# One block from attention to the experts, and batch 0's input rows reloaded in four portions

## The reference

```python
scores = einsum('bqhd,bkhd->bhqk', q, k) / sqrt(16) + slopes * -abs(pos_k - pos_q)
out = einsum('bhqk,bkhd->bqhd', softmax(scores), v) @ Wout + bout
x = layernorm(x + out)
# router: softmax over 8 logits, the top 2 kept; each expert takes its first 512 tokens
h = relu(einsum('ceh,ehi->cei', inputs, experts_inter))         # 256 -> 1024
out = einsum('cei,eih->ceh', h, experts_out) * in_w             # 1024 -> 256
x = layernorm(x + combined)
```

## Time and profile before

| | us |
|---|---|
| three runs: lowest, median, highest | 1104.36, 1107.05, 1108.21 |
| the profiled execution, its own time | 1107.38 |
| its span, first to last instruction | 1105.6 |
| attention, first score matmul to last value matmul | 116.41 to 815.35 |
| routing, first matmul to the slot table | 826.22 to 880.71 |
| experts, first gather to the end | 882.07 to 1105.6 |

### The profile page before, as it was taken

The page is one execution under the profiler, slowest core; times in us unless marked ns, Lnnn a source line. Parts: engine busy times, 40 slices in busy tenths (PEclk is TensorE's granted clock), DMA queues, the critical chain, the costliest instruction groups (busy, mean ns, idle before and its releaser), DMA issues. The chain is left out here.

```text
span 1105.6 us, 38348 instructions
## 1 busy us (share of the span) xinstructions
PE 1035.5 (94%) x16912; PEld 678.4 (61%) x16912; DVE 434.4 (39%) x1016; ACT 822.8 (74%) x832; POOL 304.1 (28%) x454
## 2 busy tenths in 40 slices
PE   7999899999999999999899999999969379999996
PEld 4555565566577584875555766857558236666665
DVE  4778234453243232234334623324236711111163
ACT  3564799999999999999799999999945255111154
POOL 2333022122112121121221521211420063654442
PEclk9999899999999999999899999999989679999998
DMA  5765312221211121214132221210216155544473
GB/s 160 226 197 167 110 49 79 56 66 58 69 58 48 49 65 38 55 44 112 65 79 55 53 71 50 64 55 15 84 32 231 61 134 174 125 114 112 110 278 122
DMA packets 76519, 104.71 MB, mean 95 GB/s; under 512 B 13743, under 2 KB 62525, under 8 KB 76349
## 3 DMA queue, kind: packets, MB, share of 16 engines
q1 hardware_dynamic: 65708, 87.94, 25.9%
q0 software_dynamic: 6080, 9.06, 4.0%
q10 hardware_dynamic: 4560, 5.19, 1.5%
HBM read 66.49 MB, written 31.48 MB: 89 GB/s over the span
## 5 line engine op out<-in xcount | busy, mean ns | idle before, releaser
L975 ACT ACTIVATE prob<-ps 128x1536 f32<-128x1536 f32 (+4 forms) x504 | 665.4, 1463 | 30.1 <-PE ps L931 28.4
L931 PE MATMUL ps<-q_stack,k_stack 99*32 99x128 bf16 (+18 forms) x8390 | 454.0, 306 | 14.8 <-ACT prob L975 6.7
L955 PE MATMUL ps<-prob,v_head 128*32 128x128 f32 (+7 forms) x7228 | 448.7, 340 | 1.0 <-DVE prob L986 0.9
L931 PEld LDWEIGHTS ps<-q_stack,k_stack 123*32 123x32 bf16 (+3 forms) x8390 | 240.8, 97 | 183.1 <-ACT prob L975 104.8
L955 PEld LDWEIGHTS ps<-prob,v_head 128*32 128x32 f32 x7228 | 253.3, 110 | 68.6 <-issue 6.4
L986 POOL TENSOR_TENSOR prob<-prob,near_bias 128x128 f32<-128x128 f32 x256 | 125.2, 493 | 539.5 <-ACT prob L975 539.2
L986 DVE TENSOR_TENSOR prob<-prob,near_bias 128x128 f32<-128x128 f32 x256 | 83.8, 334 | 439.4 <-ACT prob L975 439.2
L1004 DVE RECIPROCAL o_rec<-o_den 128x128 f32<-128x128 f32 x128 | 113.0, 922 | 0.6
L1671 PE MATMUL ps<-xeT,w 128*128 128x512 f32 x224 | 99.7, 603 | 0.8 <-ACT xeT L1703 0.7
L1685 PE MATMUL ps<-w,hT 128*128 128x256 f32 x448 | 97.8, 379 | 0.0
L1749 ACT ACTIVATE hT<-ps 128x512 f32<-128x512 f32 x28 | 16.7, 596 | 108.6 <-PE ps L1671 108.5
(11 more groups left out here) (166 smaller groups left out, 582.7 us busy)
## 6 DMA issues: line engine op xcount, KB each, us to landing
qk_parts<-split SPq DMA_DIRECT2D x32, 384.0 KB, 3.0
w<-L_ffn_experts_inter_dram SPq DMA_DIRECT2D x7, 1024.0 KB, 6.2
w<-n_L_ffn_experts_out_dram SPq DMA_DIRECT2D x7, 1024.0 KB, 9.6
q_stack<-qk_parts SPq DMA_DIRECT2D x31, 192.0 KB
k_stack<-qk_parts SPq DMA_DIRECT2D x31, 192.0 KB
z_rows<-v SPq DMA_DIRECT2D x8, 516.0 KB, 3.4
xin<-in_L_attn_x_dram ACTq DMA_DIRECT2D x8, 512.0 KB, 4.6
heads<-o_out SPq DMA_DIRECT2D x128, 32.0 KB, 2.4
```

What stands on the lines that cost most here:

```text
L931: mm = pe.matmul(ps[k:k + keys, SLOT_BANKS * (c % 2) + bank, col:col + z - a], k_st[n % STACKS][0:rows, kb * P + k:kb * P + k + keys], q_s ...
L955: mm = pe.matmul(ps[32 * g:32 * g + 32, 6 + n % 2, column:column + width * times], vh[n % 2][:, kb, :], moving, start=g not in begun, stop ...
L975: act.activation(prob[:, c % RING, 0:at + z - a], ps[:, bank:bank + SLOT_BANKS, :].rearrange("p c n -> p (c n)")[:, 0:at + z - a], ACT.Exp ...
```

## The change

There are two parts.

1. Attention, routing and experts stand in one block. The three functions return five programs each (one for an engine) and `build` runs them one after the other on each engine. Where the barriers stood there are semaphores now: `heads_ready` (raised by SP once when the outputs of batch 0 are in `heads`, again when all are), `values_taken` (raised by DVE at the end of its attention program), `y_mm`, on whose first count SP and POOL begin their routing work, and `lot_step` with `z_out` for POOL's first gather. Some buffers move so that they don't overlap; `sums` now uses the memory of `heads`. The barrier from projection to attention stays.
2. `load_rows` takes one portion (512 KB) instead of a batch. The four of batch 0 are issued in the turns n = 19, 20, 21 and 22, one at the end of each. Those of batch 1 stay where they were.

The semaphores of the rows are now used by the projection phase too, hence their higher counts.

The diff without changes of indentation:

```diff
-def load_rows(sp, b):
-    for c in range(b * QG, (b + 1) * QG):
+def load_rows(sp, c):
         sp.dma_start(t["v"][:, c * TPC:(c + 1) * TPC, 0:D], x[...])\
           .then_inc(x_in[c], 16)
...
 # banded_sync, in the loop over items n
             if n >= STACKS:
                 store_turned_heads(n - STACKS)
-            if n == H + STACKS:
-                sp.wait_ge(vh_done, H)
-                load_rows(sp, 0)
+            if 0 <= n - (H + STACKS) < QG:
+                sp.wait_ge(vh_done, H)
+                load_rows(sp, n - (H + STACKS))
+            if n == H + STACKS:
+                for buf in range(2):
+                    sp.wait_ge(o_stored[buf], 16 * GROUPS * (H // 2))
+                sp.sem_inc(t["heads_ready"], 1)
...
         for buf in range(2):
             sp.wait_ge(o_stored[buf], 16 * GROUPS * (len(ITEMS) // 2))
+        sp.sem_inc(t["heads_ready"], 1)
...
 # banded_vector, at its end
+        dve.wait_ge(o_read, len(ITEMS))
+        dve.sem_inc(t["values_taken"], 1)
...
 # routing, SyncE
+        sp.wait_ge(y_mm, 1)
         for par in range(2):
             load_expert(sp, t, w1_dram, w2_dram, par, par)
...
 # routing, TensorE
         for n in range(NCH):
+            pe.wait_ge(t["heads_ready"], n // QG + 1)
+            if n == 1:
+                pe.wait_ge(t["values_taken"], 1)
             if n >= 2:
                 pe.wait_ge(z_done, n - 1)
                 pe.wait_ge(extra_done, n - 1)
...
 # routing, GpSimd
+        pool.wait_ge(y_mm, 1)
         prefix_weights(pool, earlier, ones, const)
...
 # experts, GpSimd
+        pool.wait_ge(t["lot_step"], 4)
+        pool.wait_ge(t["z_out"], 16 * NCH)
         for e in range(2):
             gather(e)
...
 # build
-            attention_phase(nc, t, ...)
-        route_phase(nc, t, w1, w2, z_dram, ps)
-        expert_phase(nc, t, w1, w2, ...)
+            attend = attention_programs(nc, v_life, t, ...)
+            route = route_programs(nc, route_life, t, w1, w2, z_dram, ps)
+        experts = expert_programs(nc, ctx, t, w1, w2, ...)
+        with nc.Block(no_gpsimd_drain=True) as block:
+            @block.sync
+            def _(sp):
+                attend[0](sp)
+                route[0](sp)
+                experts[0](sp)
...
```

More of the change, by code:

```diff
@@ L358, in project_phase @@
         extra_done = sem("extra_done")
-        x_in = [sem(f"x_in{p}") for p in range(2)]
+        x_in = t["x_in"]
         scaled = sem("scaled")
@@ L437, in transposes @@
             def transposes(c):
-                pe.wait_ge(x_in[c % 2], (c // 2 + 1) * 16)
+                pe.wait_ge(x_in[c], 16)
                 if c >= 1:
@@ new lines, in pv @@
+                        mm = pe.matmul(ps[32 * g:32 * g + 32, 6 + b, :], vh[b][:, kb, :],
+                                       prob[:, ch % RING, c * CH:(c + 1) * CH],
+                                       start=(kb == 0), stop=(kb == KB - 1))
+                    mm.then_inc(pv_done, 1)
+                for ch in range(CHUNKS):
+                    score(ch)
+                    for kb in range(blocks_done(ch - PV_LAG - 1), blocks_done(ch - PV_LAG)):
+                        pv(kb)
+                for kb in range(blocks_done(CHUNKS - 1 - PV_LAG), KB):
+                    pv(kb)
@@ new lines, in general_scalar @@
+    def general_scalar(act):
+        act.sem_inc(expd, 2 * CHUNKS)
+        with act.Fori(0, H) as h:
+            for b in range(B):
+                for ch in range(CHUNKS):
+                    act.wait_ge(scored, h * (2 * CHUNKS) + (b + 2) * CHUNKS + ch + 1)
+                    pb, pch = ring_user_before(b, ch)
+                    act.wait_ge(pv_done, h * (2 * KB) + (pb + 2) * KB
+                                + (min(pch * SLOT_BANKS + SLOT_BANKS, TILES) - 1) // QG + 1)
+                    n = len(chunk_tiles(ch))
+                    bank = SLOT_BANKS * (ch % 2)
+                    act.activation(prob[:, ch % RING, 0:n * CH],
+                                   ps[:, bank:bank + n, :].rearrange("p c n -> p (c n)"),
+                                   ACT.Exp).then_inc(expd, 1)
@@ new lines, in general_gpsimd, with sync @@
+    def general_gpsimd(pool):
+        pool.sem_inc(vh_done, 2)
+        with pool.Fori(0, H) as h:
+            for b in range(B):
+                pool.wait_ge(pv_done, h * (2 * KB) + (b + 1) * KB)
+                pool.tensor_copy(vh[b][:, :, 0:HD], t["v"][:, b * KB:(b + 1) * KB, bass.ds(h * HD, HD)])\
+                    .then_inc(vh_done, 1)
+        for c in range(NCH):
+            add_bias(pool, c)
+    def sync(sp):
+        bounded = sp.value_load(t["bounded"][0:1, 0:1], min_val=0, max_val=1)
+        with sp.If(bounded == 1):
+            banded_sync(sp)
+        with sp.Else():
+            general_sync(sp)
@@ L2036, in build @@
         t["heads"] = ctx.enter_context(nc.sbuf_tensor("heads", [P, 2, T], F32))
+        for name in ("o_sum", "o_out"):
+            t[name] = [ctx.enter_context(nc.sbuf_tensor(f"{name}{b}", [P, CH], F32)) for b in range(B)]
+        for name in ("o_den", "o_rec"):
+            t[name] = ctx.enter_context(nc.sbuf_tensor(name, [P, CH], F32))
+        for name in ("heads_ready", "values_taken", "lot_step", "z_out"):
+            t[name] = ctx.enter_context(nc.semaphore(name))
         t["x_in"] = [ctx.enter_context(nc.semaphore(f"rows_in{c}")) for c in range(NCH)]
```

2077 lines of the change are left out of this document (1020 added, 1057 removed).

## The result

The changed kernel takes 1094.40 us (median of 4 runs, 1088.41 to 1096.49), the kernel before beside it 1107.63. The ratio is 0.9877, interval 0.9831 to 0.9923: 13.2 us less, where 1092.0 had been forecast. In two later measurements, on two chips, the ratio was 0.9908 [0.9894, 0.9923] and 0.9886 [0.9857, 0.9915], 11.1 and 11.0 us less. All three gains fall short of the 15.1 us that the sum had forecast. The profiled execution is the fastest of its four: 1088.41 us, span 1086.7 us, mean clock 0.977.

The account below looks back on a forecast made before the run. PE, busy 94% of the span, was taken as the bound, with gains only where it stands still. -6.5 - 8.2 - 0.4 = -15.1 us from 1107.38 gave 1092.3, or 1092.0 for the median; range 1087.5 to 1097.5.

Parts of the forecast that it names:

- Part 1, the reload: Attention, item 20: one portion ahead of the stack instead of four removes PE's pause and the slow clock after it, -6.5 us.
- rival 2: Attention: item 20's stack is still late and PE pauses again; 1098.5 us at worst, about 1096 for half; chance 0.11.
- Part 2, the first seam: Attention to routing: PE's first routing matmul follows its 3.62 us jump, not the barrier, so routing moves by -8.2 us.
- the flag: First seam: group 1 waits for `values_taken`; hidden if group 0 runs at half clock, up to 1.5 us shown at full clock.
- rival 3: First seam gives less: jumps and waits of several engines add up, 4 us lost over the first two groups; 1096, chance 0.08.
- falls: First seam: PE's clock falls over the 2.65 us pause with the same ramp as before, routing -8.2 us; chance 0.45.
- holds: Rival 1, first seam: the clock holds over the shorter gap, routing gains 10 to 11.5 us; 1089, chance 0.30.
- Groups 4 to 7: Routing: these groups need the last item's output in `heads`, a wait forecast as hidden by 9 us.
- POOL's constants: Routing: they run beside DVE's first adds and hold an add 1.4 us at most, covered by group 1 at half clock.
- Rival 4: Routing: PE is stopped repeatedly and runs all eight groups at half clock; slower by 8.4 us, 1115.5, chance 0.03.
- The second seam: Routing to experts: without the barrier POOL's first gather starts sooner after the slot table, -0.4 us, bounds 0 and 1.36.
- Rival 5: Merged programs don't overlap because a wait is met only when SP is through; within 3 us of before, chance 0.03.

Follow-up runs that it names:

- the early flag: Changed kernel with `values_taken` raised right behind DVE's last copy out of PSUM, not behind the last scale: 1093.66 us, ratio 0.9904.
- PE waits for all heads: Changed kernel, no barrier, but every routing group of PE waits until both batches' heads are read back: 1101.82 us, ratio 0.9960.
- one block only: Changed kernel with all four row loads ahead of item 20's stack again, the one block kept: 1096.16 us, ratio 0.9937.
- arms swapped: Changed kernel with the branch's two arms in the other order on all five engines, so the jump comes at attention's start: 1096.21 us, ratio 0.9900.
- two portions first: Changed kernel with two row loads ahead of item 20's stack and one ahead of each of the next two: 1090.35 us, ratio 0.9880.
- the fastest version: Changed kernel with `values_taken` raised behind the last PSUM copy, PE's routing and DVE's first two additions in both arms: 1087.53 us, ratio 0.9852.

## Why the prediction was nearly right

**Part 1, the reload, -6.5 us: mechanism right, size too large.** PE's wait for the stack went, as forecast, and the two profiled executions gave exactly the 6.5 us that I took from the earlier trace rows. But the two runs that measure it apart gave 3.4 us (portions added to the kernel before) and 3.9 us (portions taken from the changed kernel), and the profile of the latter has the pause at 3.07 us and 4.4 in all. I read the price from the one profile of before, which held a dear pause, and used it as if it were the median's; this is the term of the sum that was mis-sized most. Only two profiles have the pause, of two kernels and not taken side by side, so whether its price goes with the execution or with the chip isn't shown. Why the stack took 21.2 us there and 20.0 in the other, I can't say. My rival 2 (stack late) didn't happen in any run with one portion ahead.

**Part 2, the first seam, -8.2 us: mechanism right, size somewhat too large.** The first routing matmul came 8.05 us earlier relative to attention (10.86 - 2.81), as read from the jump in the earlier trace rows. Forecast for the whole seam was 42.72 - 8.2 = 34.5 us with the clock fallen, 31.1 (32.6 with the flag) with the clock held. Measured in the changed kernel and with the early flag: 35.8, 35.7 fallen, 33.6, 33.5 held. In both cases the forecast lacked the stop of 1.4 to 1.6 us behind the jump. With the clock held it lacked 0.7 us more: the matmuls of the eight groups took 1.61 + 27.56 = 29.2 us and not 28.5, since I had put the end of group 0 at DVE's first add, when PE was already in group 1. That the profiled seam (33.6) came out so near to the forecast of 34.5 is luck: the stop that I lacked and the clock that held cancel. By timed runs one block was worth 7.3 us (alone) and 7.7 us (1100.02 - 1092.31, on top of the portions), where 8.2 + 0.4 had been forecast. I had bounded the jump by its own row of 3.62 us; a seam where the jump had long been over (and the run in which PE waits for all heads) couldn't show the stop behind it. This falls under rival 3 (time lost over the first groups) at a good third of its 4 us, but not by its mechanism: DVE's jump and the adds held nothing up.

**The clock.** I chose "falls" at 0.45 over "holds" at 0.30, and the profiled execution held. In the profiles of the changed kernel and of its variants with a pause at this place it held after 2.81, 2.85 and 2.38 us, and fell after 2.58, 2.62 and 2.53. So the length of the pause doesn't decide it within this span. In the three that fell it fell only 0.6 to 1.4 us after PE had gone on. My comparison with the pause of 2.90 us at attention's start was a comparison of lengths, and had no power: that pause left the clock at half in all eleven profiles that have it, while 2.81 and 2.85 us at the seam did not. What differs between the two places wasn't tested. The Trainium skill, "TensorE: Matmul & The Clock Gate", Part 1 (The HAM clock gate), says that the observation is free-running, so that one kernel shows different numbers of slow matmuls. By that rule both cases come up by luck, and three profiles of one unedited kernel, two held and one fallen, agree; they were taken in three measurements, so by themselves they don't exclude the chip.

**The other waits of the seam** were where I had put them or smaller. `values_taken` costs nothing behind a jump, and shows at 1.35 us only when PE has no jump. Groups 4 to 7 never waited for the heads. POOL's constants stood beside the first adds (814.40 and 814.48) and nothing was late by them. The first gather waited for the slot table and not for the stored rows. Rival 4, half clock through routing, did not happen: the clock stayed, or came back within 7 us.

**The second seam, -0.4 us:** measured 0.43.

**The median.** 1092.0 was forecast and 1094.4 came. With 3.4 to 4.4 in place of 6.5 the sum would have been 1094.1 to 1095.1. Of the 15.1 us forecast, 13.2, 11.1 and 11.0 came in the three measurements; the reload was put 2.6 to 3.1 us too high, and one block 0.9 to 1.3 us. Rival 5 (nothing changes) is excluded by every ratio of the changed kernel.

## What to carry to other kernels

A pause costs what it holds up and the slow clock behind it, and both can differ from one profile to the next; before a pause of one profile is made a term of a sum, look at it in a second execution, or take a range for it. What merging two blocks saves is not so much the barrier itself as what the barrier made the next stage wait for. What comes up next is each engine's own jump over the arm that isn't taken: place that jump where the engine waits in any case, by writing the next stage's first work into both arms. An edit that only moves a jump (here: to the start of attention) moves its price with it, unless the trace shows a wait at the new place that isn't the branch itself.

## What the runs showed of the hardware that was not expected

- PE's branch not taken needs 0.09 us and the jump over the other arm 3.4 to 4.1 us. In the six profiles that have the jump right ahead of routing the pause is the jump's length less 1.0 to 1.1 us (3.86 and 2.81 in the changed kernel, 3.38 and 2.38 in the one with one block only), so the jump sets it. In the run with the arms swapped the jump takes 4.07 us:
```profile
L1216 PEldq COMPARE_BRANCH  x1: 4065/4065/4065, 117.7 to 117.7; - x1
```
- A second stop of 1.4 to 1.6 us six matmuls behind the jump, in five of these six profiles. In the sixth (two portions first) it is 0.64 us, but there the six matmuls ran at half clock and took 2.44 us instead of 1.6 to 1.7, so that the seventh starts 3.1 us after the first, as in the others (3.0 to 3.2). So what these profiles share is the time until PE can go on, and not the length of the stop. It goes with the jump, and not with the flag. That it is the fetching of code was my idea and wasn't tested.
- On DVE the row of the branch is 0.06 us, and the time shows behind it, as 2.31 us (where it is on the path) or 2.01 us (hidden) ahead of the next instruction.
- The stretch from the first gather to the end, which I held constant at 223.5 us, is 223.7 us in the changed kernel's first profile, but 1097.0 - 868.26 = 228.7 in its third and 1086.1 - 859.37 = 226.7 in the fastest version. By these profiles it goes with the chip more than with the kernel: 223.2 to 226.0 us in the four profiles of the chip on which the kernel before takes 1103.45 us, 226.8 to 229.4 in the four of the one with 1105.86, and 226.7 to 227.9 in the three of the one with 1104.80. PE's pauses around 890 us differ too:
```profile
892.09 0.73 PE L1655 MATMUL ps<-ident,xe 128*128 128x128 f32 x2 [1.51 <-ACT xe L1726]
```
```profile
890.18 0.73 PE L1665 MATMUL ps<-ident,xe 128*128 128x128 f32 x2 [3.86 <-ACT xe L1736]
```
The first row is of the changed kernel, the second of the fastest version. What sets this pause stays open, and so does what sets the length of the stretch. It is a reason to compare kernels on one chip only.
